# Setup of a two-layer graph kernel: edge fields between the copies of feature tiles, right scores stored by partition, four places for run addresses

## What is computed

```python
# layer 0: graph attention, 2 heads of 64
feat = (h @ W).reshape(N, 2, 64)
el, er = sum(feat * attn_l), sum(feat * attn_r)          # left and right scores, (N, 2)
e = leaky_relu(el[src] + er[dst], 0.2)
alpha = softmax of e over the edges of one dst
x = x + layernorm(segment_sum(alpha * feat[src], dst) + bias)
# layer 1: three hops; edges are grouped by src here
for _ in range(3):
    left = agg[src] @ q_w
    right = tanh((edge_emb[type] * agg[dst]) @ k_w)
    w = softmax of sum(left * right) over the edges of one src
    agg = normalise(segment_mean(w * edge_emb[type] * agg[dst], src))
    out += agg + entity_emb
```

## Time and profile before

| | us |
|---|---|
| three timed runs | 9760.26, 9768.52, 9771.0 |
| their median | 9768.52 |
| the profiled execution, as a run | 9773.91 |
| its span, first to last instruction | 9772.1 |
| setup up to the first group of edges, about | 850 |
| attention loop, 854 groups, about | 2150 |
| three hops with what lies between them, about | 6700 |

### The profile page before, as it was taken

How to read it: one execution, slowest core, us unless ns; L and a number is a source line. 1 busy time by engine, 2 the same in 40 slices (tenths; PEclk the granted TensorE clock), 3 DMA queues, 4 the chain that set the end, 5 groups by cost and what they waited for, 6 DMA issues and landing times.

```text
span 9772.1 us, 277606 instructions
## 1 busy us (share of the span) xinstructions
PE 8154.8 (83%) x65693; PEld 7081.5 (72%) x65693; DVE 7859.6 (80%) x33663; ACT 7236.2 (74%) x23594; POOL 6831.4 (70%) x7067
## 2 busy tenths in 40 slices
PE   7996777777775888888887888888887888888887
PEld 6985666666664777777775777777775777777775
DVE  7998999999997777777776777777776777777776
ACT  2204999999996777777776777777776777777776
POOL 1335777777775777777776777777776777777775
PEclk9998999999998999999998999999998999999998
DMA  3003444444444555555557555555557555555556
GB/s 53 5 12 78 108 109 109 108 109 109 109 106 118 157 158 159 159 159 159 158 157 149 159 159 159 159 157 158 158 157 152 160 158 157 158 157 157 159 159 132
DMA packets 1133286, 1309.57 MB, mean 134 GB/s; under 512 B 452804, under 2 KB 846874, under 8 KB 1132860
## 3 DMA queue, kind: packets, MB, share of 16 engines
q1 hardware_dynamic: 902182, 843.26, 28.2%
q0 software_dynamic: 229264, 460.98, 20.7%
q10 hardware_dynamic: 1670, 3.16, 0.1%
HBM read 1041.61 MB, written 261.38 MB: 133 GB/s over the span
## 4 chain that ended last, share of the span: by engine, by line
PE 34%; DMA 22%; issue 15%; DVE 12%; POOL 10%; ACT 4%; SPq 2%; DVEq 1%; POOLq 0%; ACTq 0%
PE bank L768 27%; DMA agg<-agg_d,arena 19%; POOL agg L730 10%; PE bank L928 2%; PE bank L913 2%; PE bank L881 2%; DVE agg L1610 2%; DVE agg L1600 2%; DVE arena L1709 2%; ACT arena L1043 2%; DMA agg<-feat_d,arena 2%; ACT arena L1123 1%; DVE arena L1686 1%; DVE arena L1590 1%; DVE arena L1568 1%
## 5 line engine op out<-in xcount | busy, mean ns | idle before, releaser
L730 POOL DMA_INDIRECT agg<-agg_d,arena x5124 | 4875.9, 952 | 1738.0 <-issue 1383.5
L1709 DVE TENSOR_TENSOR arena<-agg,bank 128x256 f32<-128x256 f32 x2562 | 1079.0, 421 | 1456.4 <-DMA agg<-agg_d,arena 1232.5
L768 PE MATMUL bank<-arena 128*128 128x129 f32 x10248 | 1766.5, 295 | 322.9 <-ACT arena L1123 314.9
L730 POOL DMA_INDIRECT agg<-feat_d,arena x1708 | 1623.0, 950 | 534.2 <-issue 436.3
L768 PEld LDWEIGHTS bank<-arena 128*128 128x128 f32 x10248 | 1382.2, 196 | 453.6 <-issue 418.9
L1119 ACT ACTIVATE arena<-arena 128x1 f32<-128x1 f32 x2562 | 755.3, 295 | 1209.4 <-DVE arena L1574 1184.7
L768 PE MATMUL bank<-tmp,wide 128*128 128x256 f32 x5124 | 1581.5, 391 | 16.9 <-DMA wide<-left_d 16.9
L768 PE MATMUL bank<-tmp,kw_s 128*128 128x256 f32 x5124 | 1570.7, 389 | 0.1
L928 PE MATMUL bank<-ident,arena 128*128 128x128 f32 x5124 | 1032.4, 284 | 553.3 <-DVE arena L1709 549.6
L928 PEld LDWEIGHTS bank<-ident,arena 128*128 128x128 f32 x5124 | 692.6, 144 | 992.2 <-DVE arena L1709 774.8
L1114 ACT ACTIVATE arena<-agg,arena 128x256 f32<-128x256 f32 x2562 | 1339.1, 523 | 54.9 <-DVE arena L1702 50.3
(11 more groups left out here) (244 smaller groups left out, 17349.0 us busy)
## 6 DMA issues: line engine op xcount, KB each, us to landing
state_d<-arena SPq DMA_DIRECT2D x488, 455.0 KB
arena<-key_d SPq DMA_DIRECT2D x489, 448.0 KB
arena<-type_d SPq DMA_DIRECT2D x367, 448.0 KB
wide<-left_d SPq DMA_DIRECT2D x2562, 64.0 KB
agg<-agg_d,arena POOLq DMA_INDIRECT x5124
agg<-feat_d,arena POOLq DMA_INDIRECT x1708
arena<-er_d SPq DMA_DIRECT2D x854, 1.0 KB
arena<-peers SPq DMA_DIRECT2D x489, 7.0 KB
```

The lines of the kernel that those rows point to most:

```text
L730: nc.gpsimd.indirect_dma_start(out=rows_r[:, k % R, c, 0:width], out_offset=None, in_=table, in_offset=bass.IndirectOffsetOnAxis(ap=peer_r ...
L768: return nc.tensor.matmul(out, lhsT, rhs, start=start, stop=stop)
L1709: V.tensor_tensor(val_r[:, j % R, :, 0:F], rows_r[:, j % R, :, 0:F], bank[0][:, 0:G].rearrange("p (c f) -> p c f", c=2), ALU.mult).then_in ...
```

## The change

It has three parts.

1. The seven edge-field instructions, `spread(0)` and `carry(0)` no longer stand ahead of the 17 tile copies on VectorE. A function `fields(t)` puts one of them behind the copy of tile 1, 3, 5, 7, 9, 11, 13, 14 and 15. The wait for the edge loads goes with the first of them, and VectorE's wait for `prefilled` moves behind the tiles.
2. `er_d` becomes a table of 128 rows (partitions) by 98 words. The store writes one piece of 392 bytes per partition instead of 49 pieces of 8 bytes. The load of a block in the attention loop reads 8 bytes out of each row, where before it read 1 KB that lay together.
3. `run_at` gets four columns, and chunk n waits for store n-4 instead of n-2.

```diff
-        er_d = dram("er_d", (NB, P, HEADS), F32)
+        er_d = dram("er_d", (P, NB * HEADS), F32)
...
-            sp.dma_start(er_d.rearrange("b p h -> p b h"), er[:]).then_inc(feat_stored, 16)
+            sp.dma_start(er_d, er[:].rearrange("p b h -> p (b h)")).then_inc(feat_stored, 16)
...
-                            sp.dma_start(er_r[:, j % U, :], er_d[bass.ds(blk, 1)].rearrange("o p c -> p (o c)")).then_inc(q["block"][j % U], 16)
+                            sp.dma_start(er_r[:, j % U, :], er_d[:, bass.ds(blk * HEADS, HEADS)]).then_inc(q["block"][j % U], 16)
...
+            def fields(t):
+
+                if t == 1:
+                    dve.wait_ge(edges_in, 9 * 16)
+                    do(V.tensor_scalar(spare_i, src_i, 7, None, ALU.logical_shift_right))
...
+                elif t == 11:
+                    do(V.tensor_tensor(spare_i, spare_i, packed, ALU.bitwise_or))
+                elif t == 13:
+                    do(V.tensor_scalar(payload[:, :, 1], spare_i, float(VALID), None, ALU.add))
+                elif t == 14:
+                    spread(0)
+                elif t == 15:
+                    carry(0)
...
-            spread(0)
-            carry(0)
-            dve.wait_ge(prefilled, 32)
             for t in range(FB):
...
+                fields(t)
+            dve.wait_ge(prefilled, 32)
...
-                if n >= 2:
-                    dve.wait_ge(run_stored, 16 * (n - 1))
-                V.tensor_copy(run_at[:, h:h + 1], ends[:, n:n + 1])
+                if n >= 4:
+                    dve.wait_ge(run_stored, 16 * (n - 3))
+                V.tensor_copy(run_at[:, n % 4:n % 4 + 1], ends[:, n:n + 1])
```

More of the change, by code:

```diff
@@ L202, in gnn_kernel @@
         ends = sb("ends", [NB, CHUNKS + 1])
-        run_at = sb("run_at", [NB, 2], I32)
+        run_at = sb("run_at", [NB, 4], I32)
         tail_at = sb("tail_at", [NB, 1], I32)
@@ L590, in _ @@
                 nc.gpsimd.indirect_dma_start(
-                    out=sorted_edges[1], out_offset=bass.IndirectOffsetOnAxis(ap=run_at[:, n % 2:n % 2 + 1], axis=0),
+                    out=sorted_edges[1], out_offset=bass.IndirectOffsetOnAxis(ap=run_at[:, n % 4:n % 4 + 1], axis=0),
                     in_=runs[:, n % 4, :], in_offset=None).then_inc(run_stored, 16)
@@ L1240, in _ @@
             scales(1, *HALVES[1])
[L1242 to L1249, removed]
+            def fields(t):
+                if t == 1:
+                    dve.wait_ge(edges_in, 9 * 16)
+                    do(V.tensor_scalar(spare_i, src_i, 7, None, ALU.logical_shift_right))
+                elif t == 3:
+                    do(V.tensor_copy(src_block, spare_i))
+                elif t == 5:
+                    do(V.tensor_copy(payload[:, :, 0], dst_i))
+                elif t == 7:
+                    do(V.tensor_scalar(spare_i, type_i, 7, None, ALU.logical_shift_left))
+                elif t == 9:
+                    do(V.tensor_scalar(packed, src_i, P - 1, None, ALU.bitwise_and))
+                elif t == 11:
[6 more added lines that the diff above has]
+                    carry(0)
             def pack(n):
```

## The result

The changed kernel takes 9743.1 us in the median of 13 runs (9737.29 to 9750.65), the kernel before 9765.26 in 13 runs beside it (9754.49 to 9771.0). The ratio is 0.9979, with a 95% interval of 0.9971 to 0.9988: 22 us less. The prediction said 9743.8.

What follows compares the result with a forecast made beforehand. No engine was taken to bound the whole kernel; stages follow each other. Gains of 8.4 (front) and 16.3 (stall) sum to 24.7 us, so 9768.5 becomes 9743.8 us, range 9735 to 9764.

Steps and rivals of the forecast that it cites:

- The front: Tile copies up to the first rank: moving the fields between copies brings ranking from 70.04 to 61.6, gain 8.4 us.
- The copy of tile 4: ScalarE's copy of transposed tile 4 in the front: expected at 40.95 instead of 51.03.
- the clock would stay at 1.00 from 40 to 110: Sign expected in the profile after: TensorE's granted clock stays at full level from 40 to 110 us.
- the two old holes: Idle times in the front: TensorE 10.08 us ahead of 48.67, and VectorE 14.89 us ahead of chunk 2's run address.
- The 0.55 for a copy with its scores: VectorE's tile copies in the front: each copy with its scores was taken to need about 0.55 us.
- The stall: VectorE's wait at chunk 2's run address for the first store: chunk 2 to 4 shrinks from 27.58 to 11.3, gain 16.3.
- the 19.9 us for the features: Feature store ahead of the first store of runs: issued at 62.1, taken to land by 82.0, 19.9 us later.
- the stall of up to 4.6 us that two places might have left: At chunk 2's run address, asked for at 77.4 with two places: the third edit is worth 0 to 4.6 us.
- Rival 1: First store of runs late by itself: stall gain 12.7, time up to 9749.4; chance 0.20 shared, for gains under 19.5.
- Rival 2: Gain eaten in the sort as chunks 4 to 15 slip: gain 16, 9752.5; chance 0.20 shared, for gains under 19.5.
- Rival 3: Attention loop: strided score loads make late gathers the rule, costing 44 us, 9788; chance in full 0.05.
- Rival 4: Nothing changes, because something behind the front sets the attention loop's start; chance 0.05, shared with mild slowing by strided loads.

Runs made afterwards that it cites:

- after_again: The changed kernel, unchanged, run once more on another chip: 9754.58 us beside 9774.7 for the kernel before, ratio 0.9979.
- er_only: The kernel before with only the score layout changed, scores stored and loaded by partition: 9760.33 us, ratio 0.9985.
- the faster front: The changed kernel with carry(0) behind the last tile copy; there, two columns of run addresses instead of four: 9738.47 us, last store 757.0 instead of 754.9.
- run4_only: The kernel before with only four columns of run addresses instead of two: ratio 0.9990.
- after_old_er: The changed kernel with scores stored and loaded by block as before, in small pieces: ratio 0.9986.

## Why the prediction was right, point by point

**The front.** Forecast 8.4, with the first rank at 61.6. It came at 61.16, 8.9 earlier, and 8.85 in after_again. The copy of tile 4 was put at 40.95 and came at 40.65; the tile pipeline absorbed the fields as worked out, and the end, with three pieces ahead of the last copy, cost what was said. The part that failed is the sentence that the clock would stay at 1.00 from 40 to 110. I had priced the slow restart behind the two old holes, and did not look whether the new end leaves TensorE idle: its last tile product was done 2.4 us ahead of the first rank, and my own numbers had that gap in them (70.04 - 0.51 - 10.5 = 59.0 for the product, 61.6 for the rank). The 0.55 for a copy with its scores was too short, since 1.53 less 0.89 of idle is 0.64; the other pieces were taken a little long, and both together came out. At chunk 2 the profiled execution had kept 83.51 - 77.81 = 5.7 of the 8.4, and after_again, without the fall, 83.51 - 74.67 = 8.8.

**The stall.** Forecast 16.3, from 27.58 to 11.3 between chunks 2 and 4. Measured 11.28. In er_only, where nothing else changed, the last store came 15.6 earlier. One term was mis-sized: the 19.9 us for the features. That was their landing with the small pieces behind them; without these they took 13.8 to 14.4 in eight executions. So they had landed at 76.1 and not at 82.0, and the stall of up to 4.6 us that two places might have left didn't exist. The score pieces landed 70.92 + 33.7 less 70.49 + 19.9 = 14.2 us behind the features, not 13.8, since they were issued 0.4 later; nothing hangs on it.

**Which part does it.** The prediction gave the score layout most of it and the third part 0 to 4.6. Measured: the layout alone 15.6, the four places alone 11.3, both with the fields 22.4 to 25.6; the four places beside the layout 0 in the changed kernel, and 2.1 with the faster front; the layout beside the four places 6.2. They are two remedies for one wait, and the layout also takes away TensorE's stops, which the prediction didn't know of. The parts' gains are not to be added: 6.9 + 15.6 + 11.3 is 33.8, and the whole is 22.4.

**Rival 1** is refuted by er_only: the first store, with the features ahead of it, lands within 6.0. The page of the Trainium skill that I had weighed (DMA: Bandwidth & Descriptors, section on queues, rings and completion order) has two sentences here. That engines go round between queues would by itself have let store 0 of the kernel before through; it didn't get through. That a semaphore increment lands behind every earlier write of its engine, across queues, agrees with 19.9 us behind the small pieces and at most 6.0 without. **Rival 2** did not occur: from chunk 4 to chunk 14 it is 58.03 us, before 58.04. **Rival 3**, in full, is refuted by the loop lengths. **Rival 4** falls with the last store: what the front gains arrives at the start of the attention loop, 21.9 of 22.4.

**The sum.** 24.7 forecast, 22.2 between the medians; 22.4 and 25.6 at the last store with and without the low clock. The predicted 9743.8 met 9743.1 partly by luck: the kernel before measured 9765.3 in more runs, 3.3 lower than the 9768.5 that I started from, and that made up for the 2.5 that I forecast too much.

## What to carry to other kernels

When a store in many small pieces goes out next to other transfers, look at who waits for those, not for it: here 49 KB of scores held up a store of another engine by some 14 us, and one contiguous piece per partition cured it. More places for the waiting address are the other remedy for the same wait; price the two together, since the second one to come may find little left. And look at what is left on the chain: the extra places hid the late store, but TensorE's stops under the small pieces stayed. When work is moved into the idle time of a pipeline, look at what stands ahead of its last stage: what the next stage doesn't need goes behind it, which shortens the start and here also kept TensorE from the gap after which its clock sometimes fell.

## What the hardware showed that I had not expected

- SyncE is busy 9.94 to 10.91 us issuing the score store in 6272 pieces (six executions), and 9.85 to 10.93 us with 128 pieces (eight). So the time doesn't go with the number of its own pieces. In all of them it stands right behind the feature store; that this is the cause was not tested. Nothing was seen to wait for it.
- With the small pieces in the queue and four places for addresses, TensorE stopped for 4.28 us (run4_only) and for 0.39 to 2.91 us (after_old_er) with nothing in the profile to wait for. The longest stop of each began at a DMA share of 1.6 to 1.8. No execution without the small pieces has such a stop between 55 and 130.
- The same kernel at the same gap of 2.39 us ahead of the first rank had its clock fall to 1.2 GHz in one execution (for 10 us) and keep 2.4 GHz in another.
- With the small pieces in the queue, the first store landed 18 to 21 us after its issue (six executions), whether this was at 74 or at 83 us, and the features 19 to 21 us after theirs; without them it was at most 6.2 and 14.4.
- One series ran all kernels at 12.9 ms instead of 9.75, with the setup at the usual pace and the loops slower (in after_old_er a mean granted clock of 0.86 from 1000 to 1500, in the changed kernel 1.00). The next series has the same chip number on record and ran at 9.75 again. Why was not looked into.
